# Fewer down-weight loads per tile, and one piece of preparation instead of two between six feed-forward slices

## What is computed

```python
xn = _layernorm(x, axis=-1)                       # x: (4, 4096, 1024)
# recurrence, M = 64
q, k, v = xn @ Wq, xn @ Wk, xn @ Wv
gates = sigmoid(xn @ Wg + bg)
S = decay * S + (k_t * g_t)[:, None] * (v_t * g_t)[None, :]   # over time
s = (q_t . S) @ Wo + bo
# FFN, HIDDEN = 3072, weights w_int / 127
h = silu(xn @ wg.T) * (xn @ wu.T)
g = silu(h @ wd.T)
out = x + s * g
```

## Time and profile before

| what | us |
|---|---|
| median of 3 executions (lowest, highest) | 714.24 (711.92, 782.95) |
| the profiled execution | 714.77 |
| its span, slowest core (3) | 713.2 |
| spans of the eight cores | 700.9 to 713.2 |
| TensorE / VectorE / ScalarE / GpSimd busy | 604.2 / 265.4 / 169.4 / 73.2 |

### The profile page before, as it was taken

One profiled execution on the slowest core, in us unless ns is written; L12 is line 12 of the kernel. 1 busy time (PEld: TensorE's weight loads), 2 busy tenths in 40 slices (PEclk: granted clock), 3 DMA queues, 4 the chain that ended last, 5 costly groups with the idle time before them and its releaser, 6 DMA issues.

```text
span 713.2 us, 8535 instructions; the slowest of 8 cores (700.9 to 713.2 us)
## 1 busy us (share of the span) xinstructions
PE 604.2 (85%) x2996; PEld 288.7 (40%) x2996; DVE 265.4 (37%) x477; ACT 169.4 (24%) x268; POOL 73.2 (10%) x146
## 2 busy tenths in 40 slices
PE   0351869598994898998899999899999999999997
PEld 0230424254551444543344444344444444444443
DVE  2367067477886325353312322211221111122222
ACT  0442074466572002211111111111111111111111
POOL 5010212211010100101000000011111111000000
PEclk9975979889997799999999999999999999999999
DMA  8970687966552331233133133165555646013132
GB/s 162 180 122 1 90 120 109 139 104 99 108 90 31 62 57 31 32 58 60 29 60 119 59 119 118 60 88 69 82 70 79 86 63 89 1 59 112 66 118 90
DMA packets 24747, 58.63 MB, mean 82 GB/s; under 512 B 2753, under 2 KB 2881, under 8 KB 24706
## 3 DMA queue, kind: packets, MB, share of 16 engines
q0 software_dynamic: 19584, 39.85, 37.2%
q1 hardware_dynamic: 4608, 16.78, 6.6%
q10 hardware_dynamic: 514, 1.45, 0.8%
HBM read 89.53 MB, written 8.39 MB: 137 GB/s over the span
## 4 chain that ended last, share of the span: by engine, by line
PE 75%; DVE 9%; DMA 6%; issue 5%; ACT 3%; POOL 1%; ACTq 0%; DVEq 0%; POOLq 0%
PE pb L712 44%; PE pb L783 23%; DVE abig L394 3%; PE pb L506 2%; DMA xstage<-xfm 2%; DMA xstage<-xpfm 2%; DVE xn L398 1%; DMA abig<-wob 1%; ACT xsqf L307 1%; DMA bgs_s<-bgs 1%; PE pb L799 1%; PE pb L423 1%; DVE wd_bf L398 1%; PE pb L326 1%; PE pb L334 1%
## 5 line engine op out<-in xcount | busy, mean ns | idle before, releaser
L712 PE MATMUL pb<-xn,gubf 128*128 128x512 bf16 x1536 | 354.6, 391 | 37.6 <-DVE xn L398 23.3
L712 PEld LDWEIGHTS pb<-xn,gubf 128*128 128x128 bf16 x1536 | 152.0, 100 | 226.4 <-issue 63.7
L783 PE MATMUL pb<-wd_bf,h_bf 128*128 128x512 bf16 x768 | 168.7, 379 | 2.7 <-DVE h_bf L739 2.7
L739 DVE SCALAR_TENSOR_TENSOR h_bf<-pb,sgbf 128x512 bf16<-128x512 f32 x96 | 66.0, 690 | 248.4 <-PE pb L712 217.2
L734 ACT ACTIVATE sgbf<-pb 128x512 bf16<-128x512 f32 x96 | 56.8, 592 | 274.8 <-PE pb L712 274.1
L783 PEld LDWEIGHTS pb<-wd_bf,h_bf 128*128 128x128 bf16 x768 | 75.0, 98 | 93.9 <-issue 3.7
L679 POOL DMA_DIRECT2D gubf<-wgu x96 | 50.9, 537 | 476.8 <-PE pb L712 366.5
L826 DVE TENSOR_TENSOR abig<-abig,pb 128x512 f32<-128x512 f32 x32 | 22.0, 687 | 130.9 <-DMA xtmt<-xtm 66.1
L817 ACT ACTIVATE abig<-pb 128x512 f32<-128x512 f32 x32 | 19.1, 598 | 160.0 <-PE pb L783 160.0
L307 ACT ACTIVATE xsqf<-xstage 128x1024 bf16<-128x1024 bf16 x32 | 31.9, 1047 | 67.3 <-DMA xstage<-xfm 33.0
L158 ACT ACT_TABLE_LOAD x32 | 41.1, 1283 | 0.6
(11 more groups left out here) (85 smaller groups left out, 205.8 us busy)
## 6 DMA issues: line engine op xcount, KB each, us to landing
gubf<-wgu POOLq DMA_DIRECT2D x96, 256.0 KB, 5.5
xtmt<-xtm SPq DMA_DIRECT2D x16, 512.0 KB, 3.9
out<-xtmt SPq DMA_DIRECT2D x16, 512.0 KB, 2.9
wd_bf<-wdt POOLq DMA_DIRECT2D x24, 256.0 KB, 10.0
xstage<-xfm POOLq DMA_DIRECT2D x8, 512.0 KB, 12.0
xstage<-xpfm POOLq DMA_DIRECT2D x8, 512.0 KB, 8.1
abig<-wqk ACTq DMA_DIRECT2D x1, 512.0 KB
xtmt<-wkvg ACTq DMA_DIRECT2D x1, 512.0 KB
```

The lines of the kernel that those rows point to most:

```text
L712: e.matmul(out=o, lhsT=gu_bf[gpar][:, gu * 1024 + dc * 128: gu * 1024 + (dc + 1) * 128], rhs=xn[:, dc * N + half * 1024 + nh * 512: dc * N ...
L739: e.scalar_tensor_tensor(out=h_bf[:, hc * 1024 + nh * 512: hc * 1024 + nh * 512 + 512], in0=a, scalar=QS, in1=sg_bf[:, sgp * 512:(sgp + 1) ...
L783: e.matmul(out=o[:, dh * 512:(dh + 1) * 512], lhsT=h_bf[:, hc * 1024 + nc2 * 128: hc * 1024 + (nc2 + 1) * 128], rhs=wd_bf[:, hc * 1024 + d ...
```

## The change

Two things are done. With each `lnA_c`, one load of down-projection weights is put into GpSimd's list in place of two; 20 blocks are loaded this way, so 16 now go with the tiles and the last 4 with the piece after them. And after each of the first six slices of the loop, one piece of `pre` is taken in place of two. An assertion checks, while the program is built, that all pieces are used when the down projection begins.

```diff
@@ build_nc, the list pre
             if k - 1 >= 0 and k - 1 < 16:
-                pre.append(lambda ti=k - 1: (lnA_c(ti), emit_wd_loads(2)))
+                pre.append(lambda ti=k - 1: (lnA_c(ti), emit_wd_loads(1)))
             if k < 16:
                 pre.append(lambda ti=k: lnA_p(ti))
         pre.append(lambda: emit_wd_loads(20))
@@ build_nc, the loop that interleaves
         for fi, fslice in enumerate(ffn[2:]):
+            if fi == 46:
+                assert pi >= len(pre), (pi, len(pre))
             fslice()
-            take = 2 if pi < len(pre) else 0
+            take = (1 if fi < 6 else 2) if pi < len(pre) else 0
```

## The result

The changed kernel takes 743.19 us (median of 10 runs, from 740.63 up), the kernel before 712.45 us in the same series; the ratio is 1.0427, with a 95% interval of 1.0396 to 1.0459. The interval leaves out one slow run of each, 764.95 and 782.95 us. The change makes the kernel slower by 30.7 us; 737 was forecast.

The account below looks back on a forecast made before the run. TensorE, busy 85% of the span, was taken to lose time in stops behind x-tile landings. Slice 27's end at 244.3 less 212.0 less 10.5 gave +21.8 us; 714.8 + 21.8 = 737 us, range 713 to 750.

Parts of the forecast that it names:

- The phase: Gate/up stage: x loads still issued after odd slices, but their Squares precede the next slice's Silu; hold-up comes 3.5 us sooner.
- The two-tile cycle: Gate/up stage with x tiles: the chain closes over two tiles in 28.15 us, later 28.65; 14.3 per tile against 10.44.
- Landing to slice: From an x tile's landing to the start of the gate/up slice it held: 12.35 us, 12.87 in the later stage.
- The landing of X 5 and X 6: Time for x tiles 5 and 6 to land with no down-weight load ahead of them: 9.1 us.
- the walk: Slice-by-slice timeline of the changed gate/up stage: slice 11 ends at 133.1 us, slice 27 at 244.3.
- the 2.5%: Taken off the four turns, 114.1 to 111.2 us, since the old cycle gave 10.7 per tile where the mean was 10.44.
- the 10.6: From issue of a gate/up weight pair to x landing, one down-weight load between: 10.6 us, middle of 12.2 and 9.05.
- What the Squares hold: On ScalarE, a tile's Squares waiting for x were said to hold up the Silu of the next slice.
- The last sign of being wrong: Stated condition for the prediction being wrong: more than the order of the Squares sets the cycle.
- Down-weight loads: One load fewer per tile for the first ten tiles: worth 1.6 us in a landing; the late loads are hidden.
- Fast landing: Rival: every x tile lands 7.3 us after the gate/up weight issue, 6.8 for tiles 5 and 6; 716 us, chance 0.14.
- Early gain kept: Rival: early lead stays, later tiles go at their old 10.44 us, needing a 4.5 us landing; 707 us, chance 0.08.

Follow-up runs that it names:

- e13: The whole change with two single pieces in place of six, preparation one slice later, pair after odd slices: 743.24 us.
- e3: The whole change with four single pieces in place of six, preparation two slices later, pair after even slices: 711.42 us.
- e4: The changed kernel with the Squares, from tile 5 on, moved on ScalarE behind the Silu of the next slice: 742.25 us.
- e8: The changed kernel with the Squares of tile t, from 5 on, moved on ScalarE behind the whole of apply t-1 (previous tile's VectorE part): 700.22 us.
- e5: The changed kernel with each x load, from tile 5 on, issued ahead of the gate/up weight pair that waits for the odd slice: 690.65 us.
- e12: The changed kernel with no down-weight loads between the tiles, all twenty behind the last tile: 735.41 us.
- e1: The kernel before with the first edit only, one down-weight load per tile in place of two: 711.67 us.

## Why the prediction was right, and where it was off

The forecast was slower by 21.8 us, the measured difference is 30.7. The time, 743.19, lies in the range and 6 us above the 737.

- **The phase** (edit 2: "X is still issued at the end of an odd slice", one slice nearer to what it holds). Right, and shown by e13, e3 and the change: odd phases at 743, even ones at 711 us, whatever the delay.
- **The two-tile cycle.** Forecast 14.3 us a tile less 2.5%, so 13.9; measured 13.9. Landing to slice: forecast 12.35 and then 12.87, measured 12.34 and then 12.86 or 12.87. Slice 11 to slice 27: 111.2 against 250.79 - 137.30 = 113.5. That the cycle comes out so well is partly luck, see the next two points.
- **Terms that were mis-sized up to slice 11.** The landing of X 5 and X 6 stood in the walk at 9.1 us; the trace has 84.59 to 95.15 and 109.43 to 119.83, so 10.6 and 10.4 (other cores come down to 8.0). With a somewhat later start (G 4 at 84.59 against 83.9) and slices after a pause of 4.9 and 5.1 us in place of 4.7, slice 11 ends at 137.3 instead of 133.1.
- **Terms that cancel in the cycle.** The four turns from slice 11 to slice 27 sum to 114.1 in the forecast, before the 2.5% are taken off, and took 113.5. The landings were 11.3, 12.0, 9.8 and 10.5 us against 10.6 each (+1.2 in all), and G was issued 0.7 us after its slice, not 0.5 (+0.8). The slice at the end of a turn was slow only once (5.8 us); in the three later turns it took 3.5 us where the sum has 4.7 (-2.6 in all). So the 2.5% had no ground, and they make up the difference between 111.2 and 113.5. Together with slice 11 that is 6.5 us: slice 27 ends at 250.8 against 244.3, and 21.8 + 6.5 = 28.3 is what the traces show lost at that place (28.4).
- **The rest of the 30.7 us.** The two profiled spans differ by 27.3. The profiled execution of before took 714.77 us, 2.3 above the median of its series, and that of the changed kernel 742.03, 1.2 below; 27.3 + 2.3 + 1.2 = 30.8. The forecast started from the 714.77.
- **Where the 10.6 came from.** I took it as the middle between no down-weight load (9.05) and two (12.2, from G at 138.88). The 12.2 is a poor sample: X 10 (the Squares at 151.12 are those of tile 10, not of tile 9 as the heading of the earlier trace rows says) was issued only at 143.33, after a wait for its buffer, and it is the shortest of its kind. X 9, also behind two loads, took 17.1 us, from 123.63 to 140.74, the longest of the six from X 5 to X 10:

```profile
123.63 1.06 POOL L679 DMA_DIRECT2D gubf<-wgu  x2 [5.86 <-PE pb L712]
...
140.74 2.00 ACT L307 ACTIVATE xsqf<-xstage 128x1024 bf16<-128x1024 bf16 x2 [2.88 <-DMA xstage<-xpfm]
...
143.33 0.53 POOL L298 DMA_DIRECT2D xstage<-xpfm  x1 [2.33 <-DVE xn L398]
```

  That 10.6 lies so near the measured 10.9 is luck, and 12.2 was not the longest that the rows allowed.
- **What the Squares hold.** The step "its Squares now stand ahead of the Silu of the next slice", taken as what decides, failed: e4 puts them behind that Silu and stays at 742 us. What decides is that they stand ahead of apply t-1 on ScalarE (e8), which keeps 8 us of VectorE's work behind the landing, together with the place of the load (e5). The last sign of being wrong that I had named, that more than the order of the Squares sets the cycle, is there. The walk had the right sum all the same, because it took the whole stretch from landing to slice out of the trace and not its parts.
- **Down-weight loads.** The 1.6 us for one load in the landing was about right (e12: 1.8 us shorter with one load less; e1: 1.9 longer with one more). That the first edit alone gives next to nothing (e1, 0.999) I hadn't worked out for itself.
- **Stats that wait for the evacuation** (15.6 us in three waits) were not in the walk. They move TensorE's stop from the slice to the stats: the later slices at the end of a turn have a pause of 1.0 to 1.3 us ahead of them in place of 5.23, and ran at 3.5 us. They don't seem to lengthen the turn: the evacuation ends with the same landing, and behind it TensorE still waits for apply t-1, 1.0 to 1.3 us each time (1.27 at 192.58). No run takes them out alone.
- **Rivals.** Fast landing: on no core did X 8 or a later tile land in under 9.1 us after G, against the 7.3 that it needed, nor X 5 or X 6 in under 8.0, against 6.8. Early gain kept: the early gain was there (at the end of slice 9, 119.94 - 4.14 = 115.8 against 122.9), but the later tiles went at 13.9, not 10.44. The landing of 4.5 us that it needed was never seen; e5 reaches 10.2 by taking the landing out of the cycle.

## What to carry to other kernels

When two lists are interleaved by hand, a shift by an odd number of places can turn the phase between a load and the thing that waits for it (one slice cost as much as three here, two cost nothing). Count for every load how many slices lie between its issue and the first *in-order* queue that stops for it, and follow that stop to the last instruction behind it on every engine. A load that stands behind another load's wait is issued when that wait ends, however long its own buffer has been free; issuing it ahead (e5, -52.5 us) or letting the work that doesn't need it go first (e8, -43 us) each break such a chain. Take a held-up stretch whole from the trace, landing to restart: here its length held (12.35 us forecast, 12.34 measured) though the reason given for it was in part wrong.

## What was not expected of the hardware

Taking bytes out of the transfer queue mattered little here: with one 256 KB load less ahead of X it landed 1.8 us sooner, and the kernel gained 7.8 of the 31 us (e12). A pause of 3 to 8 us on TensorE cost a second time. A slice right after it took 4.9 to 5.8 us where a slice takes 3.5, and where stats stood right after it they took 3.1 to 3.4 us in place of 1.75. From 161.6 to 167.5 us, in the slice after such a pause, the mean granted clock was 0.59, between the two levels (1.2 and 2.4 GHz) and near the lower; from 167.5 to 175 it was 1.00, the upper one. Over the whole span it fell from 0.949 to 0.935 with the same matmuls.
